# Shared experts by channel chunks over whole images, with their weights stationary, split and begun in the attention

## The chip, the cores and the metric

The kernel runs on one core of a Trainium2 chip. The metric is the device time in microseconds (us) of the whole program; the lower the better. TensorE (PE in the rows, with PEld for its weight loads), VectorE (DVE), ScalarE (ACT), GpSimd (POOL) and the DMA queues of SP, ACT and POOL work in parallel and meet at semaphores. A row that begins with SPq or ACTq is the issue of a DMA by that engine's queue.

## The reference, cut to what matters

Two layers run over x, 8 images of 512 tokens with 512 features. Layer 0 is a gated cross-attention to a context of 77 rows per image and a mixture of experts; layer 1 is a second cross-attention and a feed-forward part with quantised weights. The change concerns the mixture and the end of the attention ahead of it:

```python
x = x + tanh(g_xattn[0]) * attention(layernorm(x), ctx)            # 16 heads
h = layernorm(x)
logits = h @ router_w + router_b                                  # 8 routed experts
gates = softmax(logits kept at the two largest, -inf elsewhere)
expert(h, w1, w3, w2) = silu(h @ w1) * (h @ w3) @ w2              # 512 -> 256 -> 512
routed = sum over e of gates[:, e] * expert(h, routed_w[e])       # two of eight per token
shared = sum over 2 experts of expert(h, shared_w[s])             # every token
x = x + tanh(g_ffn[0]) * (routed + shared)
```

## The kernel before

There are 4096 tokens, which is 32 tiles of 128 tokens (NT), four to an image (TB). D is 512 (KD = 4 blocks of 128), HID is 256 (KH = 2), NSH = 2 shared and E = 8 routed experts. Each fp32 product is made with three passes of rounded parts, high by high, high by low and low by high (PASSES), so every operand of such a product is first split into a high part (ACT copies it, rounding) and a low part (DVE subtracts).

The program is a row of stages with a barrier between them: `attention` (first the keys and values, then 16 steps of 256 tokens, software-pipelined over s from -1 to 17), `experts`, `fuse`, `ffn`. Each engine runs its instructions in the order in which they are written.

**A step of the attention.** SP loads `xres` (two tiles of x for the residual), then `xin` two steps ahead, then stores `x1` and the normalised `xn2`. POOL adds the bias to `xres` (L461), multiplies the probabilities of the first tile by the reciprocal sums (`normalise(s, 0)`, L452), makes a reciprocal root (L445, L448) and does `normalise(s, 1)`. TensorE makes the scores (L628), the values (L658), transposes, the router's product (L677, L695), the output projection of 24 matmuls (L686), transposes of the probabilities (L638), and the next queries (L709). ACT ends its step with the copies of the transposed probabilities (L484). The DVE reads scores and projections from PSUM; it writes `xn` (L570) and `xn2` (L608).

**The stage of the experts** begins with the choices: DVE finds the two largest logits of each tile (L1081, L1084), makes one-hot rows, TensorE counts them with two matmuls (L1209), DVE makes the bounds of the experts' tiles (L1107, `bounds_done`) and the slot of each token (L1118, `slot_done`). At the same time SP loads the two shared experts' weights, ACT splits off their high parts (L1040), DVE the low parts (L1177), and the first product (L1223) waits for these.

Then 32 tiles pass through `shared(t)`. One tile is loaded and transposed with four matmuls (L1215), split by ACT and DVE (L998, L1128), and is the stationary operand of 24 matmuls of 512 columns against the weights (L1223); SiLU and gating (L965, L1133); four transposes of the gated rows (L1243), split (L969, L1139); 12 matmuls against the second weights (L1234); x1 is added (L1149) and x2 stored. In the first eight tiles ACT also reads all weights of the last stage's feed-forward part and sums their absolute values (L1011); from tile 10 on they are read again and quantised by DVE (L1167 to L1173) and stored, in 8 chunks of 1 MB.

POOL meanwhile writes zeros to the end of each routed expert's range, waits for them, and then scatters: it loads each tile of xn2 (L926) and writes it row by row to its two slots in DRAM with two indirect DMAs (L933), two tiles in flight. Only then does it fetch routed weights (L888) and split them (L894, L896) into a ring of WB = 4.

Then TensorE runs `routed(r)` over the tiles of the routed experts (69 in these data), loaded from the slots by SP, which first waits for all scatters.

## Time and profile before

| what | value |
|---|---|
| time before, median of 3 runs | 1841.53 us (1838.33 to 1842.16) |
| the profiled execution: its own time | 1842.93 us |
| its span, first to last instruction | 1841.3 us |
| PE busy | 1597.5 us (87%) |
| DVE busy | 1072.5 us (58%) |
| ACT busy | 793.6 us (43%) |
| POOL busy | 588.2 us (32%) |
| moved by DMA | 252.38 MB, mean 137 GB/s |
| mean granted clock of TensorE | 0.918 |

The busy shares are means over stages. In the profile the attention's steps run from about 77 us to 493 us, the choices and the split of the shared weights from 493 to 514 us, the shared experts to 815 us, the routed experts to about 1161 us; the rest is `fuse` and `ffn`, which the change leaves as they are. The granted clock is given as a share of TensorE's full speed: 1.00 is 2.4 GHz, 0.50 is 1.2 GHz. An idle time in brackets behind a row names what ended it.

### The profile page before, as it was taken

To read this page: it belongs to the slowest core of one execution; us is meant where nothing else is said; L and a number is where in the kernel's file an instruction comes from. 1 tells how busy PE (TensorE), PEld (TensorE's weight loads), DVE (VectorE), ACT (ScalarE), POOL (GpSimd) and SP (SyncE) were. 2 spreads that over 40 slices of the span, in tenths; PEclk is the share of its full clock that TensorE was granted. 3 is DMA by queue.
4 is the path that set the end of the run, shared out by engine and by line. 5 is a ranking of instruction groups with operands and counts; after the bars stand their busy time and mean duration, and the time that the engine had idled before them with its cause. 6 is when DMAs were issued, how large, how long until landed. Compare 5 with 4: busy or idle time off the path is not lost. (4 is left out here: it accounts for less than half of the span.)

```text
span 1841.3 us, 26082 instructions
## 1 busy us (share of the span) xinstructions
PE 1597.5 (87%) x9190; PEld 1248.2 (68%) x9212; DVE 1072.5 (58%) x1802; ACT 793.6 (43%) x1425; POOL 588.2 (32%) x544
## 2 busy tenths in 40 slices
PE   6599999999589999989999999276657899999997
PEld 5488888887368888877788888254425666666664
DVE  3568888887443445322333333378866777777775
ACT  2145444544234222223344343145545655556753
POOL 0133333333134445633420000445403443224440
PEclk9699999999589999999999999666658899999998
DMA  3112222221398898735433333687731112211102
GB/s 129 46 58 93 92 82 93 92 76 64 148 337 302 284 329 320 269 133 181 137 109 109 108 106 110 203 300 255 250 114 46 47 46 69 69 69 69 46 1 92
DMA packets 108604, 252.38 MB, mean 137 GB/s; under 512 B 15411, under 2 KB 15411, under 8 KB 104296
## 3 DMA queue, kind: packets, MB, share of 16 engines
q1 hardware_dynamic: 65656, 121.98, 19.7%
q0 software_dynamic: 17056, 67.12, 10.2%
q10 hardware_dynamic: 25808, 62.14, 9.5%
q8 instruction: 55, 0.90, 0.2%
q14 instruction: 29, 0.24, 0.0%
HBM read 147.13 MB, written 101.97 MB: 135 GB/s over the span
## 5 line engine op out<-in xcount | busy, mean ns | idle before, releaser
L1223 PE MATMUL e_u_ps<-e_w,e_xeT 128*128 128x512 f32 x1596 | 393.0, 398 | 10.5 <-DVE e_xeT L1128 10.5
L1223 PEld LDWEIGHTS e_u_ps<-e_w,e_xeT 128*128 128x128 f32 x1596 | 292.9, 188 | 73.0 <-DVE e_w L1177 8.7
L1936 PE MATMUL b_f_ps<-b_xdT,w1q 128*128 128x512 f32 x1024 | 255.1, 405 | 11.5 <-DVE b_h L1841 9.5
L1936 PEld LDWEIGHTS b_f_ps<-b_xdT,w1q 128*128 128x128 f32 x1024 | 192.1, 191 | 65.1 <-DVE b_h L1841 18.5
L1774 POOL TENSOR_TENSOR b_h<-b_h,b_srow 128x512 f32<-128x512 f32 x112 | 143.5, 1328 | 245.0 <-ACT b_srow L1795 245.0
L1234 PE MATMUL e_y_ps<-e_w,e_hT 128*128 128x512 f32 x798 | 208.3, 402 | 3.9 <-DVE e_hT L1159 2.4
L1234 PEld LDWEIGHTS e_y_ps<-e_w,e_hT 128*128 128x128 f32 x798 | 142.4, 188 | 30.4 <-issue 4.0
L1802 ACT ACTIVATE b_h<-b_f_ps,cb,cw 128x512 f32<-128x512 f32 x128 | 104.6, 817 | 123.7 <-PE b_f_ps L1936 123.4
L1838 DVE SCALAR_TENSOR_TENSOR b_h<-b_f_ps,cw,b_h 128x511 f32<-128x511 f32 x128 | 95.8, 749 | 86.3 <-ACT b_h L1802 85.9
L452 POOL TENSOR_TENSOR prob<-prob,ri 128x1232 f32<-128x1232 f32 x32 | 74.3, 2322 | 112.2 <-DVE ri L552 112.2
L1913 PE MATMUL b_o_ps<-w2q,b_h 128*128 128x512 bf16 x446 | 106.0, 393 | 2.1 <-issue 1.1
L1159 DVE TENSOR_TENSOR e_hT<-e_h_ps,e_hT 128x256 fp32r<-128x256 f32 x69 | 29.3, 424 | 127.3 <-ACT e_hT L994 127.2
L709 PE MATMUL m_ps<-xT,wq 128*128 128x256 f32 x768 | 101.0, 289 | 1.4 <-DVE xT L534 1.4
L1784 ACT ACTIVATE b_h<-b_h 128x512 f32<-128x512 f32 x128 | 87.1, 680 | 30.8 <-DVE b_h L1841 30.7
L1841 DVE SCALAR_TENSOR_TENSOR b_h<-b_f_ps,cw,b_h 128x511 f32<-128x511 f32 x128 | 96.2, 752 | 4.5
L686 PE MATMUL m_ps<-wo,oT 128*128 128x512 f32 x384 | 97.3, 410 | 0.4 <-DVE oT L575 0.4
L709 PEld LDWEIGHTS m_ps<-xT,wq 128*128 128x128 f32 x768 | 95.5, 194 | 1.8 <-DVE xT L534 1.8
L484 ACT ACTIVATE pT<-t_ps 77x512 f32<-77x512 f32 x128 | 69.0, 589 | 51.7 <-PE t_ps L638 51.7
L686 PEld LDWEIGHTS m_ps<-wo,oT 128*128 128x128 f32 x384 | 73.5, 195 | 24.2 <-issue 6.7
L1133 DVE TENSOR_TENSOR e_hh<-e_u_ps,e_sg 128x256 f32<-128x256 f32 x64 | 27.1, 423 | 104.1 <-ACT e_sg L965 104.1
L933 POOL DMA_INDIRECT slots_in_scratch<-e_srow,e_scol x64 | 70.7, 1105 | 52.8 <-DMA e_srow<-xn_scratch 33.5
L1128 DVE TENSOR_TENSOR e_xeT<-e_x_ps,e_xeT 128x512 fp32r<-128x512 f32 x101 | 69.8, 691 | 29.8 <-ACT e_xeT L998 29.7
(221 smaller groups left out, 2691.9 us busy)
## 6 DMA issues: line engine op xcount, KB each, us to landing
e_xe<-slots_in_scratch SPq DMA_DIRECT2D x69, 256.0 KB, 2.6
experts_out_scratch<-e_ye ACTq DMA_DIRECT2D x69, 256.0 KB, 2.0
xin<-in_x SPq DMA_DIRECT2D x16, 512.0 KB, 3.7
xres<-in_x SPq DMA_DIRECT2D x16, 512.0 KB, 3.8
x_scratch<-x SPq DMA_DIRECT2D x32, 256.0 KB, 2.0
xn_scratch<-xn SPq DMA_DIRECT2D x32, 256.0 KB, 2.1
e_xe<-xn_scratch SPq DMA_DIRECT2D x32, 256.0 KB, 4.3
e_fraw<-in_w1T ACTq DMA_DIRECT2D x8, 1024.0 KB, 8.0
```

The costliest lines, as they stand in the source:

```text
L452: pool.tensor_tensor(prob[:, j], prob[:, j], ri[:, j].unsqueeze(2).to_broadcast([P, H, C]), ALU.mult).then_inc(p_done, 1)
L686: mm = pe.matmul(m_bank(*u), oT[:, pa, k, j * P:(j + 1) * P], wo[:, pb, k, :], start=(k == 0 and (pa, pb) == PASSES[0]), stop=(k == KD - 1 ...
L709: mm = pe.matmul(m_bank(*u)[:, g * W2:(g + 1) * W2], wq[:, pa, k, mt * P:(mt + 1) * P], xT[:, pb, k, :], start=(k == 0 and (pa, pb) == PAS ...
L1223: mm = pe.matmul(u_ps[:, i], xeT[:, pa, k], w[:, par, pb, k * 2 * HID:(k + 1) * 2 * HID], start=(k == 0 and (pa, pb) == PASSES[0]), stop=( ...
L1234: mm = pe.matmul(y_ps[:], hT[:, pa, i * KH + k], w[:, par, pb, W1N + k * D:W1N + (k + 1) * D], start=(i == 0 and k == 0 and (pa, pb) == PA ...
L1774: pool.tensor_tensor(ht, ht, srow[:], ALU.mult).then_inc(u_done, 1)
L1784: act.activation(ht, ht, ACT.Silu).then_inc(h_done, 1)
L1802: act.activation(tile(s, m), f_ps[:, (s * KF + m) % RING], ACT.Identity, bias=cb[:, m:m + 1], scale=cw[:, m, 1:2]).then_inc(mid_tap, 1)
L1838: dve.scalar_tensor_tensor(out=ht[:, 1:S], in0=f[:, 0:S - 1], scalar=cw[:, m, 0:1], in1=ht[:, 1:S], op0=ALU.mult, op1=ALU.add).then_inc(pr ...
L1841: dve.scalar_tensor_tensor(out=ht[:, 0:S - 1], in0=f[:, 1:S], scalar=cw[:, m, 2:3], in1=ht[:, 0:S - 1], op0=ALU.mult, op1=ALU.add).then_in ...
L1913: mm = pe.matmul(o_ps[:, j % 2], rounded(s - 2, k, j), w2q[:, k, :], start=False, stop=(k == KF - 1))
L1936: mm = pe.matmul(f_ps[:, u % RING], w1q[:, k, m * P:(m + 1) * P], xdT[:, part, k], start=(k == 0 and part == 0), stop=(k == KD - 1 and par ...
```

## The change

1. **Orientation.** The shared experts are computed per image b in four chunks q of 128 hidden channels. `shared_up` makes for one chunk both halves (w1 and w3) as 128 channels by 512 tokens, 24 matmuls of 512 columns, with a 128x128 block of the weights stationary and the image's transposed tokens moving. What comes out is already transposed, so `shared_down` takes it as it is: 12 matmuls for each of the four tiles. The eight transposes per tile go. The order on TensorE is up(b,0), down(b-1), up(b,1), up(b,2), up(b,3).
2. **Transposed tokens.** The attention has them for the router (`x2T`); SP now also stores them to a scratch `xnT` in each step and loads 1 MB for each image. ACT and DVE split this image from SBUF (`x_high`, `x_low`, 2048 columns), and the gated chunk too (`h_high`, `h_low`; both inputs of `h_low` and `x_low` are in SBUF).
3. **Moved into the attention's steps 0 to 15.** SP loads in each step one of 16 chunks (512 KB) of the feed-forward weights, whose absolute values ACT sums at the end of its step, and one of 16 pieces (256 KB: 12 of the shared weights, 4 of the first image's tokens), which POOL splits right behind `normalise(s, 0)`. SP issues both ahead of `xres`, behind waits for ACT's sum and POOL's split of the step before.
4. **The attention's tail.** `shared_up` of the chunks 0 and 1 of image 0 stands in steps 16 and 17, behind the output projection and behind the values.
5. **Choices later.** They come on DVE behind the gatings of the chunks 0 and 1; the bounds behind that of chunk 3; slots and gates in the first slot of image 1. The count on TensorE is behind up(0,3).
6. **Buffers.** The scatter has four tiles in flight (GB = 4) instead of two. The ring of expert weights has 3 places instead of 4. Quantising goes in 16 chunks of half the size, one in each chunk slot of the images 1 to 4, with three buffers in and two out. x1 is loaded and x2 stored by SP, with five buffers, instead of by ACT.

```diff
+def shared_up(pe, n, xs, b, q):
+    for j in range(2):
+        first_col = j * n.HID + q % n.KH * P
+        for k in range(n.KD):
+            at = k * 2 * n.HID + first_col
+            for pa, pb in PASSES:
+                mm = pe.matmul(n.u_ps[:, (2 * q + j) % 4], n.w_shared[q // n.KH][:, pa, at:at + P], xs[:, pb, k],
...
# attention, SP
+                if 0 <= s < 2 * NC:
+                    if s:
+                        sp.wait_ge(asum_done, s)
+                    sp.dma_start(fraw[:], n.f_chunk(s)).then_inc(f_in, 16)
+                if 0 <= s < len(pieces):
+                    if s:
+                        sp.wait_ge(pre_lo, s)
...
+                    sp.dma_start(raw[:], pieces[s][2]).then_inc(raw_in, 16)
...
+                if late:
+                    sp.wait_ge(n_free, (s - 1) * 2)
+                    sp.dma_start(n.xnT_d[:, :, (s - 2) * W2:(s - 1) * W2], x2T[:]).then_inc(xnT_out, 16)
# attention, POOL
                 if mid:
                     normalise(s, 0)
+                if 0 <= s < len(pieces):
+                    split(s)
# attention, ACT, end of the step
+                    act.activation(fraw[:], fraw[:], ACT.Abs,
+                                   accum_out=n.asum[:, s // NC, s % NC:s % NC + 1]).then_inc(asum_done, 1)
# attention, TensorE
+                if s == NSTEP + 1:
+                    shared_up(pe, n, n.xs0, 0, 1)
...
+                if s == NSTEP:
+                    pe.wait_ge(s_sub, NSTEP * 4)
+                    pe.wait_ge(pre_lo, len(pieces))
+                    shared_up(pe, n, n.xs0, 0, 0)
# experts, ACT
+            for c in range(FB):
+                reload(c)
+            for b in range(B):
+                for q in range(Q):
+                    i = b * Q + q
+                    silu(b, q)
+                    if q:
+                        h_high(b, q - 1)
...
+                    if q == 1 and b + 1 < B:
+                        x_high(b + 1)
+                    if QUANT_AT < i <= QUANT_AT + 2 * NC:
+                        store_chunk(i - QUANT_AT - 1)
...
+                h_high(b, Q - 1)
# experts, DVE
+            for b in range(B):
+                for q in range(Q):
+                    i = b * Q + q
+                    if i == Q:
+                        slots()
+                        gates()
+                    if b and q == 0:
+                        for t in range((b - 1) * TB, b * TB):
+                            add_shared(t)
+                    gated(b, q)
+                    if q:
+                        h_low(b, q - 1)
+                    if b == 0 and q == 1:
+                        choices()
+                        one_hot()
+                    if b == 0 and q == 3:
+                        tile_bounds()
+                    if q == 2 and b + 1 < B:
+                        x_low(b + 1)
...
+                    if QUANT_AT <= i < QUANT_AT + 2 * NC:
+                        quantise(i - QUANT_AT)
+                h_low(b, Q - 1)
+            rx_low(0)
# experts, TensorE
+            def shared_down(b):
+                pe.wait_ge(h_lo, (b + 1) * Q)
+                for j in range(TB):
+                    t = b * TB + j
+                    if t >= 2:
+                        pe.wait_ge(x2_done, t - 1)
...
+            for b in range(B):
+                for q in range(Q):
+                    i = b * Q + q
+                    if b and q == 0:
+                        pe.wait_ge(xs_lo, b)
+                    if i >= 2:
+                        pe.wait_ge(hh_done, i - 1)
+                        shared_up(pe, n, xs[b % 2], b, q)
...
+                    if b and q == 0:
+                        shared_down(b - 1)
+            x_transposes(0)
+            shared_down(B - 1)
```

## Rows read from the trace of the kernel before

**Rows 1.** Busy time in two stretches: stretch, length, engines, clock, DMA share, GB/s

```profile
101.50:467.00 365.50, 344.37 (x3344) 292.49 (x3344) 293.49 (x452) 176.23 (x338) 130.02 (x114) 0.99 0.25 85
523.10:815.00 291.90, 287.05 (x1379) 236.07 (x1379) 122.84 (x184) 77.20 (x141) 127.14 (x141) 1.00 0.81 283
```

**Rows 2.** Timeline of the shared experts' steady tile: start, duration, engine, what

```profile
781.36 5.34 PEld L1223 LDWEIGHTS e_u_ps<-e_w,e_xeT 128*128 128x128 f32 x24
781.39 5.74 PE L1223 MATMUL e_u_ps<-e_w,e_xeT 128*128 128x512 f32 x24
...
787.29 2.60 PEld L1234 LDWEIGHTS e_y_ps<-e_w,e_hT 128*128 128x128 f32 x12
...
790.51 5.74 PE L1223 MATMUL e_u_ps<-e_w,e_xeT 128*128 128x512 f32 x24
```

**Rows 3.** Timeline of the attention's tail and the choices

```profile
474.95 7.95 PE L686 MATMUL m_ps<-wo,oT 128*128 128x512 f32 x24
...
487.49 1.97 PE L644 MATMUL t_ps<-ident,xn 128*128 128x128 f32 x8 [4.25 <-DVE xn L608]
...
493.44 2.27 DVE L1081 MAX8 e_top<-logits 128x8 f32<-128x8 f32 x32 [0.32 <-PEq L169]
...
505.69 0.17 DVE L1107 TENSOR_TENSOR e_bounds<-e_first,e_least 128x9 int32<-128x9 f32 x1
...
508.84 0.20 DVE L1118 CAST slot<-e_posf 128x64 uint32<-128x64 f32 x1
...
514.15 7.08 PE L1223 MATMUL e_u_ps<-e_w,e_xeT 128*128 128x512 f32 x24 [8.30 <-DVE e_xeT L1128]
```

**Rows 4.** Timeline: the first matmuls of the routed experts

```profile
814.99 3.00 PE L1223 MATMUL e_u_ps<-e_w,e_xeT 128*128 128x512 f32 x12 [1.50 <-DVE e_xeT L1128]
```

**Rows 5.** Groups by line and shape: busy us, mean ns of one, idle before

```profile
L1128 DVE TENSOR_TENSOR e_xeT<-e_x_ps,e_xeT 128x512 fp32r<-128x512 f32 x101 | 69.8, 691 | 29.8 <-ACT e_xeT L998 29.7
...
L608 DVE TENSOR_SCALAR xn<-x,mv,rs 128x512 f32<-128x512 f32 x32 | 43.9, 1414 | 1.2 <-POOL rs L448 1.0 <-issue 0.2
...
L969 ACT ACTIVATE e_hT<-e_h_ps 128x512 fp32r<-128x512 f32 x32 | 19.2, 599 | 81.3 <-PE e_h_ps L1243 81.3
...
L570 DVE TENSOR_SCALAR xn<-xin,mv,rs 128x512 f32<-128x512 f32 x32 | 15.9, 538 | 1.1 <-POOL rs L448 1.1
...
L1011 ACT ACTIVATE e_fraw<-e_fraw 128x2048 f32<-128x2048 f32 x8 | 15.3, 1917 | 4.7 <-issue 4.7
```

**Rows 6.** Timeline of the attention's steady step

```profile
316.42 0.44 SPq L421 DMA_DIRECT2D xres<-in_x  x1
...
319.38 1.64 PE L628 MATMUL s_ps<-k_all,qT 32*128 32x77 f32 x32
...
320.30 2.51 POOL L461 TENSOR_TENSOR xres<-xres,bo_t 128x512 f32<-128x512 f32 x2 [1.72 <-DMA xres<-in_x]
...
327.98 2.25 POOL L452 TENSOR_TENSOR prob<-prob,ri 128x1232 f32<-128x1232 f32 x1 [5.17 <-DVE ri L552]
...
333.70 1.08 PE L638 MATMUL t_ps<-ident,prob 128*77 128x128 f32 x8
...
343.39 1.07 ACT L484 ACTIVATE pT<-t_ps 77x512 f32<-77x512 f32 x2 [0.27 <-PE t_ps L638]
...
343.77 1.64 PE L628 MATMUL s_ps<-k_all,qT 32*128 32x77 f32 x32
```

**Rows 7.** DMA issues: KB each, median us from issue to landing

```profile
b_xd<-xd_scratch SPq DMA_DIRECT2D x8, 1024.0 KB, 5.7
```

**Rows 8.** Timeline of POOL: first scattered tile, routed weights fetched and split

```profile
529.56 0.58 POOL L926 DMA_DIRECT2D e_srow<-xn_scratch  x1 [9.43 <-DMA slots_in_scratch<-e_zero]
...
748.04 1.26 POOL L888 DMA_DIRECT2D e_wraw<-in_w  x1
...
759.08 2.75 POOL L894 CAST e_w<-e_wraw 128x3072 fp32r<-128x3072 f32 x1 [8.16 <-DMA e_wraw<-in_w2e]
761.91 6.83 POOL L896 TENSOR_TENSOR e_w<-e_wraw,e_w 128x3072 fp32r<-128x3072 f32 x1
```

More of the change, by code:

```diff
@@ L945, in _ @@
+            for k in range(GB):
+                send(0, k)
+            with pool.Fori(1, NT // GB) as i:
+                for k in range(GB):
+                    stage(i * GB + k, k, i * 32)
+                for k in range(GB):
+                    send(i, k)
             for e in range(NSH):
-                pool.wait_ge(ws_ready, e + 1)
                 fetch(NSH + e)
@@ new lines, in add_shared, with choices @@
+                dve.scalar_tensor_tensor(out=x2[:, t % XB], in0=y_ps[:, t % 2], scalar=tg[:, 2:3], in1=x2[:, t % XB],
+                                         op0=ALU.mult, op1=ALU.add).then_inc(x2_done, 1)
+            def choices():
+                for t in range(NT):
+                    ins = dve.max(top8[:, t], logits[:, t])
+                then(ins)
+                for t in range(NT):
+                    ins = dve.max_index(idx8[:, t], top8[:, t], logits[:, t])
+                then(ins)
@@ new lines, in slots @@
+            def slots():
+                then(dve.tensor_tensor(base[:], cum[:], tot[:], ALU.subtract))
+                then(dve.scalar_tensor_tensor(out=base[:], in0=first[:, 0:E].unsqueeze(2).to_broadcast([P, E, NT]),
+                                              scalar=float(P), in1=base[:], op0=ALU.mult, op1=ALU.add))
+                then(dve.tensor_tensor(pos[:], r_ps[:, 0].rearrange("p (t e) -> p t e", e=E),
+                                       base[:].rearrange("p e t -> p t e"), ALU.add))
+                for s in range(2):
+                    ins = dve.tensor_tensor(sel[:, s], hot[:, s], pos[:], ALU.mult)
+                then(ins)
+                then(dve.tensor_reduce(posf[:], sel[:], AX.X, ALU.add))
+                dve.tensor_copy(slot[:], posf[:]).then_inc(slot_done, 1)
@@ L1239, in h_transposes @@
[L1239 to L1256 removed]
+                mm.then_inc(ru_full, 1)
```

646 lines of the change are left out of this document (322 added, 324 removed).

## The prediction, made before the changed kernel ran

> **What bounds the kernel now.** I read the busy time by stretches first. In the attention's steps TensorE is busy 344.4 of 365.5 us, in the shared experts 287.1 of 291.9, at the full clock in both [rows 1]: it bounds both, and what the other engines do there costs only where it makes TensorE wait. Then I read the timeline of the shared experts. A tile takes 790.51 - 781.39 = 9.12 us. A matmul of 512 columns in it takes (5.34 - 2.60) / 12 = 0.228 us, from the weight loads of 24 and of 12, so 36 of them are 8.22 us and the eight transposes 0.90 us [rows 2]. Last the timeline of the seam: the last projection of the attention ends by 482.9, TensorE idles and comes back at 487.5, the choices start at 493.44, and the first shared matmul at 514.15, whose 24 take 7.08 us where the steady ones take 5.74 [rows 2, 3]. The routed experts start at 814.99 [rows 4]. Behind that point nothing in the change touches the order of the work, so the question is only how much earlier it comes. The profiled run took 1842.93 us, its span 1841.3; the median of three is 1.4 us below the former.
>
> **Tail of the attention.** 24 matmuls of chunk 0 go behind the projection, which ran up to 482.7; at 0.228 they end at 488.2. They are dense and follow dense work, so I take the full clock. The logits of step 14 wait behind them on TensorE, and the DVE's in-order queue makes the last `xn2` wait for those logits: it comes at 490 and not 487.5, under chunk 1 (488.7 to 494.2). Then the tail that took 493.44 - 487.49 = 5.95 us follows [rows 3]; its eight transposes took 1.97 us, slower than at the full clock, so I take 5.0. The last store of the transposed tokens lands about when the logits are done. The stage ends at 499.3, 5.9 us later than before.
>
> **Head of the next stage.** Chunks 2 and 3 need the gating of chunk 0: ACT issues three loads (0.5 us each as an estimate from SP's 0.44 [rows 6]), loads its table (I allow 1.3), SiLU of 512 columns 0.6, DVE 0.7 [rows 5]: 4.35 us with the barrier, so TensorE starts at 503.65. The split of the shared weights, and the choices, which held it until 514.15, are off this path. I leave 1.3 us for a slow clock at this start, as 7.08 against 5.74 shows [rows 2, 3]. On DVE: gatings of 0 and 1, `h_low`, then the choices and one-hot rows, about 8.4 us, until 513.5; gating, `h_low` and `x_low` (4 x 0.69 at most [rows 5]) until 517.3. TensorE is through chunk 3 and the count at 516.6: a stall of 0.7. Bounds took 505.86 - 493.44 = 12.4 us of DVE in all [rows 3], now with the gatings between them they come at about 521.9, 16 us later; slots at 525.9, before TensorE's third down tile needs the first x2.
>
> **The stage itself.** 32 tiles x 36 less the 48 of the tail leave 1104 matmuls. Their count and their columns are what they were; only which operand stands still is exchanged. At 0.228 they take 252.0, at 0.253 (transposes free, all of 9.12 us put on 36) 279.7. I take 0.230, since the row's own difference is the nearer evidence: 253.9 us. Transposes removed: 29 us over 32 tiles. To that the count 0.6; the last chunk's SiLU, gating, high and low part with nothing else for TensorE, 2.4; the last addition 1.2. Sum: 503.65 + 253.9 + 1.3 + 0.7 + 0.6 + 2.4 + 1.2 = 763.8. Against 814.99 that is 51 us earlier.
>
> The Trainium skill, "TensorE: Matmul & The Clock Gate", section on the back-to-back issue gap, gives an isolated warm gap of N / 2.4 + 2.5 ns, 215.7 for 512 columns. By it, as an estimate, the 1104 would take 238 us, 16 less than I take. The rows show 228, and I stay with the rows.
>
> **Other engines in the stage.** An image takes 33.1 us. DVE does four gatings, four low parts, `x_low`, four additions, and in images 1 to 4 four chunks of quantising (1.9 us each as an estimate, three passes over 1024 columns): under 20 us. The load isn't even: chunks 1, 2 and 3 are 5.5 us apart. In slot 2 DVE has 0.7 + 0.7 + 2.8 + 1.9 = 6.1, and `h_low` of chunk 3, which the down product needs 5.5 us after chunk 3's matmuls, is ready at 5.2. That is tight; I put 0 to 2 us per image on it, 2 in all. ACT has under 12 us.
>
> GpSimd's split of the first routed weights (2.75 + 6.83 us [rows 8]) now falls beside low parts whose two inputs lie in SBUF. The rows show such an effect: the same 512 columns cost DVE 538 ns at L570, and 1414 at L608, beside POOL's multiplication [rows 5, 6]. I allow one stall, 1 us in the sum, 6.8 at most. The Trainium skill, "SBUF — State Buffer", "Who interferes with whom", says that a VectorE instruction with two SBUF inputs shuts out, or waits whole for, a GpSimd one that reads SBUF. By that rule the stall would be the whole instruction, the upper bound of the sentence before; the two groups of rows agree with it in kind.
>
> **Attention steps.** A step is 343.77 - 319.38 = 24.39 us. POOL's split of 512 columns is a sixth of rows 8, 1.6 us, in a gap of 5.2 to 5.8 us behind `normalise`. ACT's sum is 1.2 us (half of L1011 and the readout) where ACT is idle. Neither is on TensorE's path. The waits on SP are the point. `xres` was issued at 316.42 and landed at 320.30; now it is issued after ACT's sum and behind two other loads, at 344.46 + 1.2 + 0.9, 5.8 us later in the step (322.2 in the earlier one). With 768 KB ahead of it: 512 KB took 3.9 us and 1 MB 5.7 [rows 6, 7], so 768 KB more add 2.7 at most, and they start 0.9 earlier: landing within 3.9 to 5.7. Taking 5.7: 327.9, addition 2.5, `normalise` 2.25, 332.7, and TensorE asks at 333.70 [rows 6]. One us is left. I take 1 us in all for the attention.
>
> **Scatter.** It starts with the bounds, 16 us later: 545.6. It took 748.04 - 529.56 = 218.5 us, and the first routed weights were ready 20.7 later, at 768.74 [rows 8]. TensorE wants them at 764. The pace must therefore rise. Two tiles in flight took 13.7 us a pair, of which some 5.2 are POOL's four indirect issues. With four in flight the same waits are paid half as often: 8 x (10.4 + 8.5) = 151 us. The bandwidth: 283 GB/s at 0.81 share is 349 at most [rows 1]; x, x1, x2 and quantising take about 190, which leaves at 0.95 share 141 GB/s for 25 MB: 178 us. By that bound it ends at 724 and the weights are ready at 744, 20 us ahead.
>
> **Sum.** 51.2 - 2 - 1 - 1 = 47 earlier: 1842.9 - 47 = 1796 for a profiled run, 1794.5 for a median.
>
> **Rivals.** (A) *The scatter becomes the bound.* For it: it ran at a DMA share of 0.81, and four in flight doesn't make bandwidth. At the old pace the weights are ready at 545.6 + 218.5 + 20.7 = 784.8, 21 us late: 1815. Against it: the stage moves 11 MB less than before. (B) *The matmuls aren't as cheap with weights stationary*, and the transposes were nearly free: 0.253 each, 26 us lost: 1820. (C) *The end on the other side: `xres` stretches every step.* The loop is 10.8 us from TensorE's question to ACT's last copy, 1.2, 0.9, the landing L, 2.5, 2.25 and 0.3: 17.9 + L, against 24.4. Above L = 6.5 every us costs 15. At 8 the result is 1817; above 9.7 the kernel is slower than before. Against it: such a landing needs more than twice 3.9 at a DMA share of 0.25 [rows 1]. (D) *DVE comes late in quantising images*, 4 us in each of four: 1809.
>
> **Chances.** Forecast 0.62, its own range 1787 to 1801. A 0.12, B 0.06, C 0.10, of which 0.03 slower and 0.02 no change, D 0.10. Range for all: 1784 (both rates low, no stall, a shorter tail) to 1817. Within 0.2%, which is about what these runs can tell from no change, 0.02; slower 0.03; faster 0.95.
>
> **What would show it.** Right: about 33 us per image in the shared stage, no transposes; TensorE dense from 475 to 494; about 4 us from the barrier to chunk 2; attention steps of 24.4 us; the routed weights split before 750. Wrong: `prob` (L452 before) released by the `xres` load; the first routed matmul waiting for POOL's split or for the slots' load; TensorE waiting for `h_low` before each down product.

## The result, and the profile after

The changed kernel took 1792.99 us in the median of four runs (1791.89 to 1800.59), against 1840.05 for the kernel before beside it (1838.33 to 1842.16). The ratio is 0.9753, with a 95% interval of 0.9722 to 0.9783. The prediction was 1794.5. The profiled execution took 1793.91 us, its span 1792.4, at a mean clock of 0.921.

The timeline of the changed kernel from the attention's last projection to the first down product, which answers to [rows 3]:

```profile
474.65 7.68 PE L773 MATMUL m_ps<-wo,oT 128*128 128x512 f32 x24
...
482.16 5.65 PE L196 MATMUL e_u_ps<-e_xs,w_shared 128*128 128x512 f32 x24
...
488.01 5.74 PE L196 MATMUL e_u_ps<-e_xs,w_shared 128*128 128x512 f32 x24
...
498.98 0.56 SPq L958 DMA_DIRECT2D e_xs<-xn2T_scratch  x1
...
501.84 1.09 ACT L1076 ACTIVATE e_sg<-e_u_ps 128x512 f32<-128x512 f32 x2
...
503.22 14.05 PE L196 MATMUL e_u_ps<-e_xs,w_shared 128*128 128x512 f32 x48 [5.97 <-DVE e_sg L1175]
...
517.49 5.70 PE L196 MATMUL e_u_ps<-e_xs,w_shared 128*128 128x512 f32 x24
523.02 11.04 PE L1322 MATMUL e_y_ps<-w_shared,e_hT 128*128 128x512 f32 x48
```

`shared_up` (L196) stands in the tail twice. The stage of the experts begins at 498.98, the first SiLU runs at 501.84, behind three issued loads and a table load, and chunks 2 and 3 follow. Before, the first shared matmul came at 514.15 [rows 3]. The 48 matmuls of these two chunks took 14.05 us; the row below shows what 48 take at the full clock.

The same timeline further on, which answers to [rows 2] and [rows 4]:

```profile
620.94 11.04 PE L1322 MATMUL e_y_ps<-w_shared,e_hT 128*128 128x512 f32 x48
631.82 21.92 PE L196 MATMUL e_u_ps<-e_xs,w_shared 128*128 128x512 f32 x96
...
748.46 11.20 PE L1322 MATMUL e_y_ps<-w_shared,e_hT 128*128 128x512 f32 x48 [1.80 <-DVE e_hT L1181]
760.50 3.01 PE L1338 MATMUL e_u_ps<-e_w,e_xs 128*128 128x512 f32 x12 [0.85 <-DVE e_x L1187]
764.68 0.65 PE L1330 MATMUL e_s_ps<-ident,e_xe 128*128 128x128 f32 x4 [1.16 <-DMA e_xe<-slots_in_scratch]
```

An image is now 48 down matmuls and 96 up matmuls without a gap: 653.58 - 620.94 = 32.64 us, where the next down product began at 653.58. That is 0.2267 us per matmul. The routed experts start at 760.50, 54.5 us earlier than at 814.99 [rows 4].

Busy time by stretches, with the columns of [rows 1]:

```profile
101.50:467.00 365.50, 342.90 (x3334) 291.55 (x3329) 293.51 (x452) 191.37 (x366) 159.94 (x146) 0.99 0.41 138
508.00:760.00 252.00, 249.85 (x1102) 206.18 (x1100) 125.92 (x231) 50.88 (x72) 119.02 (x145) 1.00 0.84 305
```

TensorE bounds the attention and the shared stage as before. The attention moves 138 GB/s where it moved 85, and the shared stage 305 where it moved 283 [rows 1]. Neither makes TensorE wait in this execution: the last projection starts at 474.65, where it started at 474.95 [rows 3], and in the shared stage TensorE waits for no load.

The attention's steady step, which answers to [rows 6]:

```profile
320.21 1.64 PE L713 MATMUL e_u_ps<-k_all,qT 32*128 32x77 f32 x32
...
323.54 0.43 SPq L487 DMA_DIRECT2D xres<-in_x  x1
...
328.39 2.55 POOL L538 TENSOR_TENSOR xres<-xres,bo_t 128x512 f32<-128x512 f32 x2 [8.94 <-DMA xres<-in_x]
...
330.89 2.25 POOL L529 TENSOR_TENSOR prob<-prob,ri 128x1232 f32<-128x1232 f32 x1
...
334.53 1.08 PE L723 MATMUL t_ps<-ident,prob 128*77 128x128 f32 x8
...
344.68 1.64 PE L713 MATMUL e_u_ps<-k_all,qT 32*128 32x77 f32 x32
```

The step is 344.68 - 320.21 = 24.47 us. `xres` is issued at 323.54, landed by 328.39 (4.85 us), and the normalising that waits behind it on GpSimd ends at 333.14, 1.39 us before TensorE asks at 334.53.

GpSimd, which answers to [rows 8]:

```profile
550.76 0.58 POOL L1035 DMA_DIRECT2D e_srow<-xn_scratch  x1 [14.74 <-DMA slots_in_scratch<-e_zero]
...
702.34 0.58 POOL L998 DMA_DIRECT2D e_wraw<-in_w  x1
...
717.67 7.13 POOL L1005 TENSOR_TENSOR e_w<-e_wraw,e_w 128x3072 fp32r<-128x3072 f32 x1
```

The scatter runs from 550.76 to 702.34: 151.6 us, where it took 218.5 [rows 8]. The first routed weights are split by 724.80, 35.7 us ahead of their use.

### The profile page after: what moved, and what is told of

Its sections match the earlier page's. It is cut to its first block and busy times, and to the rows that moved or that the text cites. A ratio compares the mean times of both kernels' runs of the same rounds, so it can differ in the third digit from the quotient of the medians.

```text
span 1792.4 us, 24986 instructions
## 1 busy us (share of the span) xinstructions
PE 1565.5 (87%) x8934; PEld 1221.4 (68%) x8956; DVE 1057.7 (59%) x1767; ACT 777.5 (43%) x1384; POOL 614.0 (34%) x576
## 5 line engine op out<-in xcount | busy, mean ns | idle before, releaser
L196 PE MATMUL e_u_ps<-e_xs,w_shared 128*128 128x512 f32 x768 | 179.2, 394 | 6.0 <-DVE e_sg L1175 6.0
L196 PEld LDWEIGHTS e_u_ps<-e_xs,w_shared 128*128 128x128 f32 x768 | 146.1, 191 | 36.6 <-DVE e_sg L1175 6.1
L1338 PE MATMUL e_u_ps<-e_w,e_xs 128*128 128x512 f32 x528 | 133.3, 401 | 2.0 <-DVE e_xs L1267 1.2
L1338 PEld LDWEIGHTS e_u_ps<-e_w,e_xs 128*128 128x128 f32 x528 | 95.8, 188 | 23.3 <-DVE e_xs L1267 1.6
L1275 DVE TENSOR_TENSOR e_hT<-e_r_ps,e_hT 128x256 fp32r<-128x256 f32 x69 | 29.3, 425 | 126.5 <-ACT e_hT L1115 126.5
L538 POOL TENSOR_TENSOR xres<-xres,bo_t 128x512 f32<-128x512 f32 x32 | 40.6, 1291 | 150.3 <-DMA xres<-in_x 150.3
L1076 ACT ACTIVATE e_sg<-e_u_ps 128x512 f32<-128x512 f32 x32 | 19.0, 598 | 168.2 <-PE e_u_ps L196 168.1
L563 ACT ACTIVATE pT<-t_ps 77x512 f32<-77x512 f32 x128 | 69.0, 589 | 51.2 <-PE t_ps L723 51.2
L1322 PE MATMUL e_y_ps<-w_shared,e_hT 128*128 128x512 f32 x384 | 88.5, 390 | 1.8 <-DVE e_hT L1181 1.8
L773 PEld LDWEIGHTS m_ps<-wo,oT 128*128 128x128 f32 x384 | 72.2, 191 | 23.7 <-issue 6.6
L628 DVE TENSOR_REDUCE mx<-e_u_ps 128x8 f32<-128x616 f32 x64 | 49.9, 779 | 62.1 <-PE e_u_ps L713 62.1
```

What stands on the lines that cost most here:

```text
L196: mm = pe.matmul(n.u_ps[:, (2 * q + j) % 4], n.w_shared[q // n.KH][:, pa, at:at + P], xs[:, pb, k], start=(k == 0 and (pa, pb) == PASSES[0 ...
L773: mm = pe.matmul(m_bank(*u), oT[:, pa, k, j * P:(j + 1) * P], wo[:, pb, k, :], start=(k == 0 and (pa, pb) == PASSES[0]), stop=(k == KD - 1 ...
L1322: mm = pe.matmul(y_ps[:, t % 2], hT[:, pa, q, j * P:(j + 1) * P], w[e][:, pb, at:at + D], start=(q == 0 and (pa, pb) == PASSES[0]), stop=( ...
L1338: mm = pe.matmul(u_ps[:, 0], xeT[:, pa, k], w[par][:, pb, k * 2 * HID:(k + 1) * 2 * HID], start=(k == 0 and (pa, pb) == PASSES[0]), stop=( ...
```

## Experiments

All kernels below are the changed kernel with one edit, unless said otherwise. Three groups of four were run, each on a chip of its own; ratios are to the kernel before on that chip. Single runs of one kernel differ by 5 to 19 us, so the stage in which an edit acts is read from its trace, which is one execution, and the whole time only from groups of four to six runs. For the traces I use two distances: **head**, from the start of the attention's last projection (474.65 above) to the first down product (523.02): 48.4 us in the changed kernel; and **stage**, from there to the first routed matmul (760.50): 237.5 us.

### The changed kernel again (same_again)

> The changed kernel once more, unaltered, as the measure for the three kernels that run beside it. Expected: 1793 us again within 0.3%, TensorE's first matmul of the experts' stage at about 503.2 us, its first routed matmul at about 760.5, tile 1 of the routed experts waiting for its load from the slots.

1805.38 us in the median (1798.45 to 1806.93, 5 runs), ratio 0.9777 (0.9751 to 0.9804). The routed matmuls began at 770.35 and not at 760.50. The head took 47.3 us, but the stage 246.7 instead of 237.5. The place is one row of the timeline:

```profile
714.10 2.76 POOL L1003 CAST e_w<-e_wraw 128x3072 fp32r<-128x3072 f32 x1 [9.14 <-DMA e_wraw<-in_w2e]
...
714.97 9.55 DVE L1181 TENSOR_TENSOR e_hT<-e_sg,e_hT 128x512 fp32r<-128x512 f32 x2
...
716.94 7.03 POOL L1005 TENSOR_TENSOR e_w<-e_wraw,e_w 128x3072 fp32r<-128x3072 f32 x1
...
724.58 13.59 PE L1322 MATMUL e_y_ps<-w_shared,e_hT 128*128 128x512 f32 x48 [4.88 <-DVE e_hT L1181]
```

`h_low` (L1181, two instructions in the row) starts at 714.97 and ends at 724.52, just behind GpSimd's subtraction (716.94 + 7.03 = 723.97). A single `h_low` takes 0.69 us elsewhere. TensorE waits 4.88 us for it, and its next 48 matmuls take 13.59 us instead of 11.04, with the granted clock at 0.83 from 720 to 740. In the first profile of the changed kernel the same place reads

```profile
714.30 3.84 DVE L1181 TENSOR_TENSOR e_hT<-e_sg,e_hT 128x512 fp32r<-128x512 f32 x2
...
714.50 3.08 POOL L1003 CAST e_w<-e_wraw 128x3072 fp32r<-128x3072 f32 x1 [9.97 <-DMA e_wraw<-in_w2e]
```

GpSimd's conversion (L1003, the high part) takes part in it, too. In same_again it began at 714.10, ahead of the first low part, which so took 2.43 us and ended 0.54 us behind it; the second low part then stood behind the subtraction and took 7.20. In the changed kernel's first profile the first low part came first (714.30, before 714.50). The second took 3.06 us, ended at 718.14, 0.56 us behind the conversion, and nothing was left for the subtraction (717.67) to hold up: the down product began at 718.86 without a wait. So both executions met the same obstacle. They differ by which of two instructions came first, by less than a microsecond.

### The tail off (no_tail)

```diff
-                if s == NSTEP + 1:
-                    shared_up(pe, n, n.xs0, 0, 1)
...
-                if s == NSTEP:
-                    pe.wait_ge(s_sub, NSTEP * 4)
-                    pe.wait_ge(pre_lo, len(pieces))
-                    shared_up(pe, n, n.xs0, 0, 0)
...
                     if i >= 2:
                         pe.wait_ge(hh_done, i - 1)
-                        shared_up(pe, n, xs[b % 2], b, q)
+                    shared_up(pe, n, xs[b % 2], b, q)
```

> The two chunks of image 0 that are computed in the attention's tail are computed at the start of the experts' stage instead; all else stays. My theory: the 48 matmuls fill TensorE's idle time of the tail and of the stage's head, but they also push the last steps of the attention 5.9 us back, so they are worth little: the stage begins near 493.1, its first matmul near 494.5, chunks 0 and 1 are through by 506.5 (11.0 at the full clock, 1 for the slow start), and chunk 2 begins there, where it begins at 503.2 now: 2 to 4 us slower in all, 0.1 to 0.2%. Rival 1: their whole 11.0 us of TensorE time is what the tail gains, so the kernel gets 11 us slower. Rival 2: the slow clock that chunks 2 and 3 show now (14.05 us for 48 matmuls instead of 11) comes from the idle time between tail and head, so without the tail it is dearer still: 48 matmuls at up to 20 us, 8 us slower or more.

1806.84 us (1797.93 to 1810.33), ratio 0.9782 (0.9754 to 0.9811): not to be told from same_again by the whole time. The timeline:

```profile
475.65 7.56 PE L771 MATMUL m_ps<-wo,oT 128*128 128x512 f32 x24
...
494.14 24.70 PE L196 MATMUL e_u_ps<-e_xs,w_shared 128*128 128x512 f32 x96 [0.93 <-PEq L208]
...
526.71 3.56 PE L1316 MATMUL e_y_ps<-w_shared,e_hT 128*128 128x512 f32 x15
```

The head takes 526.71 - 475.65 = 51.1 us, 2.7 more than in the changed kernel and 3.8 more than in same_again. The 96 matmuls of image 0 run in 24.70 us, 2.8 over the full clock's 21.9. So the 48 matmuls in the tail are worth 2.7 to 3.8 us, which is what my theory had (2 to 4), and not their whole 11; and the slow clock costs 2.8 us without them, where it cost 3.0 (14.05 less 11.04). Both rivals fall.

### The choices in front (choices_first)

```diff
+            choices()
+            one_hot()
             for b in range(B):
...
-                    if b == 0 and q == 1:
-                        choices()
-                        one_hot()
```

> The choices and one-hot rows go back in front of the first gating on the DVE; the rest stays. My theory: the first gating then waits for the choices (about 8 us from 499.3), TensorE's chunk 2 begins near 508.3 instead of 503.2, so 5 us slower (0.28%), and the bounds and with them the scatter come some microseconds earlier, which gains nothing since the scatter ends 58 us ahead of the first routed matmul. Rival: the choices weren't on the path (the start of the stage waits for something else): no change at the first matmul and none at the end. Second rival: the longer idle time makes the clock fall for longer, and the cost is 8 us or more.

1810.22 us (1797.64 to 1816.36), ratio 0.9808 (0.9776 to 0.9841), against 0.9777 for same_again: unclear in the whole time. In the timeline chunk 2 starts at

```profile
508.61 13.43 PE L196 MATMUL e_u_ps<-e_xs,w_shared 128*128 128x512 f32 x48 [10.81 <-DVE e_sg L1175]
...
527.78 2.43 PE L1321 MATMUL e_y_ps<-w_shared,e_hT 128*128 128x512 f32 x10
```

which is 33.5 us behind the projection's start instead of 28.6. The head is 527.78 - 475.15 = 52.6 us, 4.3 to 5.3 more: my theory's 5.

### The split late again (late_split)

no_tail, and at the stage's start also:

```diff
+            for e in range(NSH):                                     # SP
+                for dst, src in n.weights(e, wraw[:, e]):
+                    sp.dma_start(dst, src).then_inc(fq_out[e], 16)
+                act.activation(w[e][:, 0], wraw[:, e], ACT.Copy).then_inc(w_hi, 1)      # ACT
+                dve.tensor_tensor(w[e][:, 1], wraw[:, e], w[e][:, 0].bitcast(F32), ALU.subtract).then_inc(w_ready, 1)  # DVE
+                    if i in (0, KH):                                 # TensorE
+                        pe.wait_ge(w_ready, i // KH + 1)
```

> As no_tail, and besides the shared experts' weights are loaded and split again at the start of the experts' stage, by ACT and DVE, as the kernel before did, and the first products wait for that split. (The splits in the attention stay, so its steps are the same.) My theory: the first load lands some 7 us after the stage's start at 493, ACT needs 2.7 us for the high part and the DVE about 3.4 for the low one, so up(0,0) begins near 507 where it began at 494.1 in no_tail, and the first down product near 540 instead of 526.7: 13 us from the moved split, and up to 3 more from a clock that has fallen in the idle time. Rival: the DVE's choices and gatings for image 0 are the longer chain at the head, and the late split hides behind them: under 5 us.

1812.88 us (1810.31 to 1816.98), ratio 0.9844 (0.9822 to 0.9866), against 0.9775 for the changed kernel on that chip.

```profile
504.42 3.36 DVE L1280 TENSOR_TENSOR w_shared<-e_wraw,w_shared 128x3072 fp32r<-128x3072 f32 x1 [12.73 <-ACT w_shared L1127]
...
507.83 23.85 PE L196 MATMUL e_u_ps<-e_xs,w_shared 128*128 128x512 f32 x96 [16.36 <-DVE w_shared L1280]
...
539.59 11.04 PE L1326 MATMUL e_y_ps<-w_shared,e_hT 128*128 128x512 f32 x48
```

The first matmul waits for the split until 507.83, and the head takes 539.59 - 473.96 = 65.6 us (the last projection began at 473.96), 14.6 more than no_tail. The rival (hidden behind the DVE's work) falls. The moved split is the largest part of the head's gain.

### Transposes put back (transposes_back)

```diff
+                    if 2 <= b < B - 1:
+                        for _ in range(8):
+                            pe.transpose(x_ps[:, 1], ident[:], ident[:])
                     for q in range(Q):
```

> The changed kernel with eight transposes of 128 columns in front of each tile's down product in images 2 to 6: 160 in all, of the identity and into a free part of PSUM, which nobody reads. They stand for the transposes that the change took away. My theory: each costs what the eight of a tile cost before, 0.90 / 8 = 0.11 us, so an image takes 36.3 us instead of 32.7 and the stage 18 us more. Rival (B of the prediction): the transposes ran nearly free between the matmuls and it was the matmuls that cost more with the tokens stationary; then the 160 cost under 8 us.

1811.45 us (1809.6 to 1814.52), ratio 0.9838 (0.9816 to 0.9859). Two images' starts of the up products:

```profile
566.62 21.93 PE L196 MATMUL e_u_ps<-e_xs,w_shared 128*128 128x512 f32 x96
...
602.89 21.93 PE L196 MATMUL e_u_ps<-e_xs,w_shared 128*128 128x512 f32 x96
```

An image takes 602.89 - 566.62 = 36.27 us instead of 32.64, so one transpose costs 3.63 / 32 = 0.113 us. 160 make 18.1 us; the stage took 255.5 us, 18.0 over 237.5. The whole time rose by only 0.0063 x 1841 = 11.6 us against the changed kernel on the same chip. The profiles agree with that: the changed kernel's had a collision like that of same_again in its stage (245.7 us), and this one's cost TensorE nothing: 255.5 - 245.7 = 9.8.

### A shorter head (shorter_head)

```diff
-            sp.wait_ge(xnT_out, 16 * NSTEP)          # end of the attention; now ahead of the load of image 2
+                if s == NSTEP + 1:                   # ACT, end of the attention
+                    act.activation(fraw[:, 0:1], fraw[:, 0:1], ACT.Silu)
-            for c in range(FB):
-                reload(c)
...
+                    if i == 1:                       # ACT, behind the second SiLU
+                        for c in range(FB):
+                            reload(c)
+                    sp.wait_ge(rx_full, 1)           # SP, ahead of the last four stores of x2
+                    sp.dma_start(xe[:], n.tile_rows(n.xs_d, 1)).then_inc(xe_in, 16)
```

> Five waits taken out. (1) The attention no longer ends with the wait for the stores of the transposed tokens; the stage of the experts waits for them before it loads image 2. (2) ACT loads its SiLU table at the end of the attention with a one-column SiLU. (3) ACT issues the three loads of feed-forward weights behind the first two SiLUs, not ahead of them. (4) The load of tile 1 of the routed experts is issued as soon as tile 0 is transposed, and not behind the last four stores of x2. My theory: the stage begins 1.5 us earlier (497.5), the first SiLU starts 0.5 us behind it and not 2.9, chunk 2 begins near 499.3 instead of 503.2; the routed phase gets 2 to 3 us shorter at its first tiles. Together 6 us, 0.3%, and up to 2 us more from the clock. Rival: the time gained at the head is given back, since image 0's DVE work (choices, bounds, low parts) then makes chunk 3 or the first down product wait: 3 us in all, from the routed tiles alone.

1803.11 us (1799.13 to 1813.01), ratio 0.9778 (0.9748 to 0.9807): no difference from same_again. But each edit did its work where it stands:

```profile
476.01 7.69 PE L776 MATMUL m_ps<-wo,oT 128*128 128x512 f32 x24
...
501.31 13.97 PE L197 MATMUL e_u_ps<-e_xs,w_shared 128*128 128x512 f32 x48 [2.71 <-DVE e_sg L1183]
...
516.66 5.74 PE L197 MATMUL e_u_ps<-e_xs,w_shared 128*128 128x512 f32 x24 [1.01 <-DVE e_xs L1176]
522.24 8.10 PE L1330 MATMUL e_y_ps<-w_shared,e_hT 128*128 128x512 f32 x35
...
790.67 2.90 PE L1356 MATMUL e_y_ps<-e_w,e_hT 128*128 128x512 f32 x6 [1.30 <-DVE e_hT L1283]
```

Chunk 2 starts 25.3 us behind the projection instead of 28.6. Of that, 1.01 us comes back as a wait for `x_low` at 516.66, and the 48 matmuls take 13.97 us; the head is 46.2 us, 1.1 to 2.1 less. The stage took 247.3 us with a wait of 5.35 for `h_low`, GpSimd's instruction having started at 715.97. The fourth routed tile starts 784.37 - 769.58 = 14.8 us behind the first, where it took 779.47 - 760.50 = 19.0 in the changed kernel: 4.2 us gained. The next product then waits 1.31 us for a load and 1.30 for a low part, and runs at a slow clock (2.90 us for six matmuls of 1.64). By the fifth tile nothing of the 4.2 is left.

### GpSimd's subtraction in six pieces (small_split)

```diff
-                pool.tensor_tensor(w[ring][:, 1], wraw[:, par], w[ring][:, 0].bitcast(F32), ALU.subtract).then_inc(w_ready, 1)
+                for c in range(0, WN, D):
+                    last = pool.tensor_tensor(w[ring][:, 1, c:c + D], wraw[:, par, c:c + D], w[ring][:, 0, c:c + D].bitcast(F32),
+                                              ALU.subtract)
+                last.then_inc(w_ready, 1)
```

> GpSimd splits off the low part of each routed expert's weights in six instructions of 512 columns instead of one of 3072; all else is the changed kernel. In the profile of same_again that one instruction took 7.03 us (716.94 to 723.97) and the DVE's h_low of chunk 3, both of whose inputs lie in SBUF, ended only behind it: TensorE waited 4.88 us for the next down product, whose 48 matmuls then took 13.59 us instead of 11.04. In the profile of the changed kernel the same split started at 717.67, after h_low, and cost nothing. My theory: the two instructions shut each other out whole, and the split falls on an image's end or not by chance, from one execution to the next. With small pieces h_low waits at most 1.2 us: no wait over 1.3 us at a down product, 237 to 239 us from the first down product to the first routed matmul in every execution (246.7 in same_again), and this kernel's runs up to 8 us below those of same_again, with less spread. Rival: the DVE is late by itself at that place (choices or quantising behind it), and the small pieces change nothing but add GpSimd time.

1798.48 us (1794.9 to 1802.48), ratio 0.9734 (0.971 to 0.9759).

```profile
709.75 10.92 POOL L1006 TENSOR_TENSOR e_w<-e_wraw,e_w 128x512 fp32r<-128x512 f32 x6
...
712.75 3.38 DVE L1171 TENSOR_TENSOR e_xs<-e_xs 128x2048 fp32r<-128x2048 f32 x1
...
763.42 3.06 PE L1341 MATMUL e_u_ps<-e_w,e_xs 128*128 128x512 f32 x12 [0.84 <-DVE e_x L1190]
```

The six pieces and the DVE's low parts now pass in turn: the pieces need 10.92 us instead of 7, `x_low` 3.38 instead of 2.29, and what TensorE loses there is 0.5 us (an up group of 96 in 22.40 instead of 21.92). The stage takes 237.9 us. The whole time doesn't show the gain by itself: the changed kernel wasn't run on this chip, and xres_first beside it (below), whose GpSimd instruction is whole and did meet a low part, has 0.9725. What the pieces gain is read from the traces.

The stage in the other profiles supports it. Single-instruction kernels with a wait: same_again 246.7 us, no_tail 246.1 (5.70 for `x_low`), choices_first 241.3 (1.93), shorter_head 247.3, xres_first 244.8 (2.85), xres_late 244.9 (4.16), late_split 244.6 (3.72), same_on_this_chip 245.7 (4.04). Without: the changed kernel's own profile, 237.5, and transposes_back, where one low part took 2.25 us at the subtraction's end (717.93 to 720.18) and TensorE had no need of it yet.

Not all of these stages' length is the collision. Undisturbed, one down product follows the other after 32.64 us, and the last after 29.61. By these distances the collision cost 2.2 us (choices_first) to 8.6 (no_tail), its slow clock included; with the six pieces it is 0.5 here and 0.8 in combined. Another 1.6 us is a slow clock at the last down product, with the collision (same_again, shorter_head, xres_first, late_split, same_on_this_chip) and without it (combined). And choices_first and xres_first lost 1.6 and 1.3 us in the images 4 and 5, ahead of GpSimd's split, where the DVE was late; I haven't found why.

### xres ahead of the new loads, and behind xin (xres_first, xres_late)

```diff
                 if back:
                     sp.dma_start(xres[:], n.tile_rows(n.x, (s - 1) * 2, 2)).then_inc(xres_in, 16)
# xres_first: these two lines stand ahead of the loads of fraw and raw and of their waits
# xres_late: these two lines stand behind the load of xin
```

> In the attention SP issues the load of xres ahead of the two new loads and their waits (512 KB of feed-forward weights, 256 KB of a piece), as the kernel before had it. My theory: TensorE waits for nothing that this load sets, so the step stays at 24.46 us, and the whole kernel within 0.2%, though xres lands some 3 us earlier. Rival: the later landing costs each step a few tenths through the DVE's order (addition, statistics, second sum); then the steps fall to 24.39 or less and 1 us or more is gained.

1797.54 us (1794.12 to 1802.77), ratio 0.9725 (0.9698 to 0.9751), not to be told from small_split beside it. The step is 345.19 - 320.72 = 24.47 us, unchanged. Its `shared_up(0,0)` came at 477.77, 4.4 us earlier than in the changed kernel: from 468 to 478 its granted clock was 1.00, where it was 0.50 in the changed kernel and in same_again, behind the same wait for GpSimd of 4.0 us. xres_late has it as well: its last projection takes 5.86 us, as here, and those of the changed kernel's and the ten remaining profiles 7.5 to 8.0. I can't say how the place of this load would set the clock. The ratio is 0.5% below the changed kernel's on the two other chips (0.9777 and 0.9775), more than the 0.2% that I expected at most; since the changed kernel wasn't run on this chip, a gain isn't shown, nor is it ruled out.

> In the attention SP issues the load of xres behind the one of xin, not ahead of it, in every step. It comes 2.4 us later in the step (325.9 instead of 323.54), with 512 KB more ahead of it. My theory (rival C of the prediction, forced): the normalising of the second tile's predecessor ends at 333.14 and TensorE asks at 334.53, so 1.4 us of slack; beyond that every microsecond lengthens the step. Expected: a step of 25.4 to 26.5 us instead of 24.46, TensorE waiting for GpSimd's prob, 15 to 30 us slower in all. Rival: the order on GpSimd has more slack than the rows show, or the xin load behind was what slowed xres: no change.

1825.34 us (1822.14 to 1834.5), ratio 0.9898 (0.9864 to 0.9932).

```profile
340.65 0.47 SPq L490 DMA_DIRECT2D xres<-in_x  x1
...
345.72 2.55 POOL L538 TENSOR_TENSOR xres<-xres,bo_t 128x512 f32<-128x512 f32 x2 [12.46 <-DMA xres<-in_x]
...
348.22 2.25 POOL L529 TENSOR_TENSOR prob<-prob,ri 128x1232 f32<-128x1232 f32 x1
...
350.57 1.07 PE L723 MATMUL t_ps<-ident,prob 128*77 128x128 f32 x8 [0.86 <-issue]
...
360.61 1.64 PE L713 MATMUL e_u_ps<-k_all,qT 32*128 32x77 f32 x32
```

The load lands 5.07 us after its issue, the normalising ends at 350.47 and TensorE starts at 350.57: it is now released by it. The step is 360.61 - 334.95 = 25.66 us, and `shared_up(0,0)` starts at 499.57, 14.8 to 17.4 us later than in the profiles with 482.16 to 484.73. Those profiles had a slow clock in the last projection, which this one hadn't; against xres_first, which hadn't either, it is 499.57 - 477.77 = 21.8 us. By the ratios it is (0.9898 - 0.9776) x 1841 = 22 us slower than the changed kernel in its two groups, and 32 slower than xres_first on the same chip; the profiled run was the fastest of its four.

### Two tiles in flight (two_in_flight)

```diff
-    GB = 4
+    GB = 2
```

> The scatter has two tiles in flight (GB = 2) instead of four; all else is the changed kernel. In the changed kernel the scatter took 151.6 us (550.76 to 702.34), in the one before 218.5. My theory: the pace is set by the waits for each group of tiles, so with two in flight it needs about 218 us again, ends near 769, the first routed weights are ready near 790 and TensorE waits for them: 25 to 30 us slower (1820). Rival: the pace is set by the DMA's bandwidth, and the scatter is faster now since the stage moves fewer bytes beside it; then two in flight do 151 to 175 us, and the time stays.

1815.62 us (1809.69 to 1821.72), ratio 0.9818 (0.9789 to 0.9847).

```profile
758.36 0.58 POOL L998 DMA_DIRECT2D e_wraw<-in_w  x1
...
760.18 0.33 SPq L980 DMA_DIRECT2D e_xe<-slots_in_scratch  x1
...
768.52 1.11 PE L1330 MATMUL e_s_ps<-ident,e_xe 128*128 128x128 f32 x4 [22.08 <-DMA e_xe<-slots_in_scratch]
```

The scatter took 758.36 - 550.91 = 207.5 us, so its pace is that of the waits, and the rival of the bandwidth falls: four in flight save 56 us of it. TensorE waits 22.08 us. But not for the split weights, as I had expected: SP's load of slot tile 0 (760.18) stands behind the waits for the scatter, and TensorE transposes that tile ahead of the last down product. The last 48 shared matmuls wait with it. In the whole time only (0.9818 - 0.9776) x 1841 = 8 us are lost against the changed kernel in its two groups, and not the 25 to 30 that I expected. Part of the difference may be that GpSimd's split now falls behind these up products (768.48), so this stage has no collision up to its last product.

### Both together (combined, same_on_this_chip)

shorter_head and small_split in one kernel.

> The edits of shorter_head and of small_split together. My theory: at the head chunk 2 begins 25.3 us behind the start of the attention's last projection, as in shorter_head (28.6 in the changed kernel), of which 1 to 2 us come back as a wait for x_low before up(1,0); from the first down product to the first routed matmul it takes 238 us, as in small_split, with no wait over 1.3 us; at the routed tiles 1 to 3 some 4 us are gained, and they stay gained, since no GpSimd instruction over 2 us stands beside the low parts. In all 3 to 8 us under the kernel of same_on_this_chip by the medians, and less spread. Rival: the gains are refunded once more, by DMA waits of the routed tiles and by the clock: no difference that can be measured.

> The changed kernel unaltered, as the measure for the three beside it. 1793 to 1806 us. By my theory of the split that collides, its profile shows either no wait at the down product of image 5 or 6 and about 237.5 us from the first down product to the first routed matmul, or one of up to 7 us, followed by matmuls at half the clock, and 241 to 247 us.

combined: 1793.49 us (1788.66 to 1795.91, 5 runs), ratio 0.9736 (0.9716 to 0.9756). The changed kernel beside it: 1802.32 (1793.64 to 1803.02, 5 runs), ratio 0.9775 (0.975 to 0.98). By the ratios combined is 0.4% faster, about 7 us, with intervals that overlap in their last 0.06%: likely, not certain, and the two edits' shares aren't separated by it.

```profile
713.69 5.74 PE L197 MATMUL e_u_ps<-e_xs,w_shared 128*128 128x512 f32 x24 [0.45 <-DVE e_xs L1179]
...
762.53 3.02 PE L1349 MATMUL e_u_ps<-e_w,e_xs 128*128 128x512 f32 x12 [0.84 <-DVE e_x L1198]
```

The head is 46.1 us (476.59 to 522.68) and the stage 239.9, with 0.45 us of waiting at 713.69. In same_on_this_chip `x_low` was the victim: `h_low` of chunk 1 was shut out for 6.50 us (708.86 to 715.36, GpSimd's instruction 708.03 to 714.81), `x_low` came behind it, and up(7,0) waited 4.04 us.

## Why the prediction was right, and where it wasn't

**The matmuls and the transposes.** I took 0.230 us per matmul of 512 columns; it was 0.2267, so the 1056 from up(1,0) on took 3.5 us less. The transposes' 29 us hold: 0.113 us each in transposes_back, as in [rows 2]. Rival B is refuted. By the isolated gap that the Trainium skill gives, "TensorE: Matmul & The Clock Gate", section "Back-to-back issue gap", it would have been 215.7 ns; the trace does not agree (227).

**Tail and head.** Barrier predicted at 499.3, measured 498.98; chunk 2 at 503.65, measured 503.22; the first down product's predecessor up(1,0) at 517.3 by my terms, measured 517.49. Two terms were off and partly cancelled: 1.3 us for the slow clock was 3.0 (14.05 less 11.04), and the stall of 0.7 at up(1,0) was nil. That the slow matmuls gave the DVE the time for it fits the other profiles: in same_again the 48 took 12.51 us and the stall was 0.22, and with shorter_head, where chunk 2 starts 3.3 us sooner behind the projection, it was 1.01. The three causes of the gain at the head, undone one by one, are 14.6 us for the early split, 4.3 to 5.3 for the late choices, 2.7 to 3.8 for the tail's two chunks: 21.6 to 23.7, if they add up. The kernel before comes near that: its first shared matmul came 514.15 - 474.95 = 39.2 us behind the projection [rows 3], that of no_tail 494.14 - 475.65 = 18.5, so 20.7 for the first two, where the single steps give 18.9 to 19.9.

**Other engines.** The DVE's 2 us of lateness didn't come in the changed kernel's first profile: in the images with quantising `h_low` was ready 1.1 us ahead. (choices_first and xres_first lost 1.6 and 1.3 us there.) The collision with GpSimd's split I had put at 1 us, 6.8 at most. In the changed kernel's first profile it cost nothing, and in eight of ten later profiles with that instruction whole it was there, at 2.2 to 8.6 us. This is the term that I mis-sized. I had priced the stall alone; TensorE's clock falls behind it too (48 matmuls in 13.59 us), and so the 4.88 us of waiting in same_again became 4.88 + 2.55. The rest of its 9.2 is mostly a slow clock at the last down product (12.78 us instead of 11.20), which combined shows too (12.81), without the collision. The rule of the Trainium skill, "SBUF — State Buffer", "Who interferes with whom", that such instructions wait whole for each other, is borne out: 9.55 us for two low parts, ending just behind GpSimd's subtraction. I had also overlooked the conversion ahead of the subtraction: it held a low part up in five profiles, until some 0.55 us behind its own end. What is shown is that a GpSimd subtraction of 7 us beside a DVE subtraction with both inputs in SBUF costs this, and that the two profiles with six short ones lost under 1 us.

**Attention steps.** Right to the half microsecond: the normalising ended at 333.14 (predicted 332.7), 1.39 us were left (predicted 1), and the step was 24.47 (24.39 before). Rival C was real: with the load issued 2.37 us later in the step, of which 1.39 was slack, each step got 1.2 us longer (0.98 beyond the slack, and a landing later by 0.22). The attention lost 21.8 us by it against xres_first, which is 18 per us of a step, where I gave 15.

**Scatter.** It started 5.2 us later than predicted (550.76 against 545.6): the writing of zeros took 27.3 us (523.50 to 550.76), where it took 22.1 before (507.49 to 529.56). Its duration was 151.6, my estimate from latencies 151; in the other profiles with four in flight it was 143 to 152. The bound by bandwidth (178) was too careful. Rival A was a wait of 22 us for two in flight, near the 21 I gave, but by another chain, that of the load of tile 0.

**Behind the shared stage a step failed.** "Behind that point nothing in the change touches the order of the work": it does. The routed experts started 54.5 us earlier, where I had 51.2, but their last product only 51.2 earlier (1108.43 against 1159.66 before). The timeline of SP shows the place:

```profile
752.32 8.49 SPq L967 DMA_DIRECT2D x_scratch<-e_x  x4
762.06 0.37 SPq L989 DMA_DIRECT2D e_xe<-slots_in_scratch  x1
```

x2 is now stored by SP (L967) and no longer by ACT. The load of routed tile 1 (L989) stands behind the last four stores, the fourth of which waits for the last addition, and is issued at 762.06. TensorE waits 1.16 us for that tile and 1.19 for its low part. shorter_head issues it earlier, and the waits of the first tiles shrink to 0.50 and 0.48 us. But that this order costs the whole 3.3 us isn't shown. From the first routed matmul to the last product it took 347.9 us, where it took 344.7 before; shorter_head and combined, with the load early, still take 347.2 and 347.5. What they gain at the first tiles they lose at the next ones, and where the 3 us come from stays open. The point is still one I should have asked of each queue: what stands behind the moved instruction.

Another 2.3 us were lost in the last stage: its first 80 up matmuls took 20.83 us, 18.95 before, and its clock was 0.82 against 0.86 in its first 70 us. In same_again the same group took 18.93 and in same_on_this_chip 20.44, so this varies between executions.

**Sum.** -54.5 at the routed start, +3.3 in the routed tiles, +2.3 in the last stage: -48.9 of span; predicted -51.2 + 2 + 1 + 1 = -47. The 4 us of reserves that I had taken off were needed, though for other things than I named. So the 1.5 us between forecast and median are in part luck: the matmuls were cheaper than I took them, the work behind them dearer, and the profiled run lost nothing to the collision. In the two later groups the ratio was 0.9777 and 0.9775, which is 1800 us for a kernel before of 1841.53; that is inside the range of 1787 to 1801, at its upper end.

## What to carry to other kernels

When work is spread evenly over engines, look for the one long instruction: a GpSimd subtraction of 7 us in SBUF shuts out the DVE's short ones, and whether it hits changed from one execution to the next; look at more than one profile, and try it in pieces. When a DMA is moved to another queue, list what stands behind it there, at the seam to the next stage above all. A split or a load that only the first product of a stage needs is worth moving ahead (14.6 us here); filling TensorE's gap at a seam with matmuls gives back little of their length (3 to 4 of 11 us) when the chain of the other engines goes on behind them.

## What the runs showed of the hardware

- Two subtractions with both inputs in SBUF, one on GpSimd and one on the DVE, don't overlap: a DVE instruction of 0.69 us took 6.50 and ended 0.55 us behind GpSimd's (same_on_this_chip). GpSimd's conversion of 3072 columns ahead of it did the same: a low part took 2.43 us beside it (same_again). Cut into six, GpSimd's took 10.92 us instead of 7 and the DVE's 2048 columns 3.38 instead of 2.29 (small_split).
- A wait of 4 to 6 us on TensorE cost 1.5 to 3 us more in the matmuls behind it (7.99 us for 24 at 717.62 in same_on_this_chip, 5.74 at the full clock; behind the same wait of 5.97 us 48 took 14.05 in the changed kernel and 12.51 in same_again, 11.04 at the full clock).
- The scatter's pace with four tiles in flight was 18.9 us per four, with two 13.0 per two.
